# Ranges and one-hot rows of a sparse attention layer: from VectorE's comparisons to ScalarE's absolute values and positive parts

## What is computed

```python
mask = adj.astype(jnp.float32) + jnp.eye(n, dtype=jnp.float32)
q, k, v = [(h @ W.T + b).reshape(n, 8, 32) for W, b in ((Wq, bq), (Wk, bk), (Wv, bv))]
scores = jnp.einsum('nhd,mhd->hnm', q, k) / jnp.sqrt(32)
scores = jnp.where(mask[None, :, :] == 0, -1e9, scores)
attn = jax.nn.softmax(scores, axis=-1)
ctx = jnp.einsum('hnm,mhd->nhd', attn, v).reshape(n, 256)
h1 = _layer_norm(h + ctx @ Wo.T + bo, ln1_g, ln1_b)
ff = jax.nn.relu(h1 @ W1.T + b1) @ W2.T + b2
h2 = _layer_norm(h1 + ff, ln2_g, ln2_b)
```

## Time and profile before

| | us |
|---|---|
| median of 3 runs | 682.92 |
| lowest and highest of them | 676.41, 685.6 |
| the profiled execution, its own time | 665.67 |
| its span in the trace | 663.7 |
| PE busy in it | 530.3 |
| DVE busy | 478.3 |
| POOL busy | 238.9 |
| ACT busy | 170.1 |
| mean granted clock of TensorE, as a share of full speed | 0.903 |

### The profile page before, as it was taken

One profiled execution on the slowest core, in us unless ns is written; L12 is line 12 of the kernel. 1 busy time (PEld: TensorE's weight loads), 2 busy tenths in 40 slices (PEclk: granted clock), 3 DMA queues, 4 the chain that ended last, 5 costly groups with the idle time before them and its releaser, 6 DMA issues.

```text
span 663.7 us, 7651 instructions
## 1 busy us (share of the span) xinstructions
PE 530.3 (80%) x2434; PEld 420.0 (63%) x2434; DVE 478.3 (72%) x1210; ACT 170.1 (26%) x357; POOL 238.9 (36%) x368
## 2 busy tenths in 40 slices
PE   6979679886797988789889785587858598989791
PEld 5868567775466748646775672366745368577680
DVE  1659687898885997999789798989985996412000
ACT  1111122212321341242224133111213213521610
POOL 5100033634331465446452434324351524122222
PEclk9989769989698999899789998678978889999896
DMA  9974689999886689686645527066672753020100
GB/s 332 409 302 161 230 309 327 406 347 339 325 285 229 217 317 336 200 341 239 253 134 207 206 58 259 19 244 244 223 236 66 262 182 110 18 64 0 33 16 19
DMA packets 39211, 141.08 MB, mean 213 GB/s; under 512 B 4856, under 2 KB 15352, under 8 KB 35072
## 3 DMA queue, kind: packets, MB, share of 16 engines
q1 hardware_dynamic: 24176, 94.90, 38.7%
q0 software_dynamic: 13328, 43.55, 19.2%
q10 hardware_dynamic: 1664, 2.11, 1.0%
HBM read 123.74 MB, written 16.80 MB: 212 GB/s over the span
## 4 chain that ended last, share of the span: by engine, by line
PE 43%; DVE 33%; issue 8%; DMA 7%; ACT 5%; POOL 3%; DVEq 0%; POOLq 0%; ACTq 0%
PE ps L1009 12%; PE ps L1021 10%; DVE found L485 8%; PE ps L990 4%; PE ps L980 3%; DMA adj_buf<-in_adj 3%; DVE stats L1075 2%; PE ps L1555 2%; PE ps L814 2%; PE ps L1573 2%; DMA work<-q_table,row_of 2%; PE ps L777 2%; DVE slots L674 2%; PE ps L815 1%; ACT early L1065 1%
## 5 line engine op out<-in xcount | busy, mean ns | idle before, releaser
L485 DVE FIND_INDEX8 found<-ones,adj_buf 128x8 uint32<-128x4105 int32 (+19 forms) x54 | 145.2, 2689 | 0.0
L1009 PE MATMUL ps<-xT_all,w 128*128 128x512 f32 (+1 forms) x288 | 129.5, 597 | 11.1 <-ACT xT_all L1055 10.0
L1021 PE MATMUL ps<-w,xT_all 128*128 128x256 f32 x512 | 121.9, 393 | 3.6 <-ACT xT_all L1055 2.7
L1021 PEld LDWEIGHTS ps<-w,xT_all 128*128 128x128 f32 x512 | 98.8, 198 | 17.7 <-ACT xT_all L1055 3.6
L1009 PEld LDWEIGHTS ps<-xT_all,w 128*128 128x128 f32 x288 | 57.2, 208 | 60.4 <-issue 45.4
L940 POOL DMA_INDIRECT slots<-kv_table,col_of x54 | 54.2, 1004 | 63.8 <-DVE col_of L558 52.2
L1075 DVE BATCH_NORM_STATS2 stats<-ps 128x6 f32<-128x256 f32 x64 | 22.9, 419 | 64.0 <-PE ps L980 64.0
L1555 PE MATMUL ps<-early,xT_all 128*128 128x256 f32 x256 | 63.6, 413 | 6.1 <-DMA early<-in_wqkvT 6.0
L1055 ACT ACTIVATE xT_all<-ps,col_table 128x512 f32<-128x512 f32 (+1 forms) x72 | 45.4, 642 | 71.5 <-PE ps L1009 65.7
L1555 PEld LDWEIGHTS ps<-early,xT_all 128*128 128x128 f32 x256 | 53.3, 210 | 14.8 <-DMA early<-in_wqkvT 6.0
L814 PE MATMUL ps<-work,slots 128*128 128x128 f32 x160 | 34.8, 327 | 28.8 <-DVE slots L683 28.8
(11 more groups left out here) (160 smaller groups left out, 885.1 us busy)
## 6 DMA issues: line engine op xcount, KB each, us to landing
adj_buf<-in_adj SPq DMA_DIRECT2D x32, 2048.0 KB
xT_all<-in_xT SPq DMA_DIRECT2D x15, 512.0 KB, 22.0
kv_table<-slots POOLq DMA_DIRECT2D x7, 1024.0 KB, 5.0
slots<-kv_table SPq DMA_DIRECT2D x12, 512.0 KB
q_table<-slots POOLq DMA_DIRECT2D x16, 256.0 KB
out_dram<-early SPq DMA_DIRECT2D x7, 512.0 KB
q_own<-q_table SPq DMA_DIRECT2D x12, 256.0 KB
slots<-kv_table SPq DMA_DIRECT2D x8, 256.0 KB
```

The costliest lines, as they stand in the source:

```text
L485: last = nc.vector.max_index(dst, ones8[:], part)
L1009: last = nc.tensor.matmul(ps[:, q["bank"] + f % 2, 0:q["g"] * P], w1[:, k, f * P:(f + 1) * P], q["h1T"][:, k, :], start=(k == 0), stop=(k ...
L1021: nc.tensor.matmul(to, q["ffT"][:, f, j * P:(j + 1) * P], w2[:, f, :], start=(f == 0), stop=False)
```

## The change

For all batches but tile 0, ACT makes both matrices alone. Ranges: the distance as before, then max(0, distance + b) with b = 0.5 - spill/2 (so the constants of `half` at L521 change), then max(0, 1 - that), in place, each pass waiting for the one before. With half-integer distances this gives exactly 1 inside the range and 0 outside. One-hot rows: |column + 0.5 + (128 t - node number)|, the bracket being made by one new subtraction of 128xU on DVE in `cols_dve`, then max(0, 1 - that), in place. Tile 0 keeps its comparisons on DVE under new names. `rt_act` stands where `distance_act` stood; `onehot_act` stands behind the exponential of the step (in the head, behind evacuation 11). The waits of the readers follow: `lists_pe` and `ell_pe` wait for ACT's semaphores. POOL makes the constant `tile_mid` with two more instructions.

```diff
@@ spill_dve
-            nc.vector.tensor_scalar(units(half, q), units(spill, q), 0.5, -0.25, ALU.mult, ALU.add)
+            reach = (0.5, -0.25) if q.first else (-0.5, 0.5)
+            nc.vector.tensor_scalar(units(half, q), units(spill, q), reach[0], reach[1], ALU.mult, ALU.add)
@@ rt_dve, now for tile 0 alone
-        def rt_dve(dve, q):
-            dve.wait_ge(distance, q.p + 1)
+        def rt0_dve(dve):
+            q = TILE0
+            dve.wait_ge(distance, total_prepared(two_signals, q.p + 1))
...
@@ cols_dve
+            done = total_prepared(two_signals, q.p)
+            if not q.first:
+                mids = tile_mid[:, q.tiles[0]:q.tiles[0] + q.T]
+                nc.vector.tensor_tensor(row_off[q.par][:, 0:q.U], mids if q.nu == 1 else mids.to_broadcast([P, q.U]), got[:, :, q.k + 1],
+                                        ALU.subtract).then_inc(slots_ready, 1)
@@ onehot_dve, now for tile 0 alone, without its wait for acc_ps
-        def onehot_dve(dve, q):
...
+        def onehot0_dve(dve):
@@ lists_pe
-            pe.wait_ge(rt_ready, q.p + 1)
+            if q.first:
+                pe.wait_ge(scoring0, 1)
+            else:
+                pe.wait_ge(rt_ready, q.b + 1)
             pe.wait_ge(starts_ready, q.p + 1)
-            wait(pe, onehot_ready, q.p)
+            wait(pe, cols_ready, q.p)
+            if q.p == TILE0.p + 1:
+                pe.wait_ge(scoring0, 2)
@@ ell_pe
-            pe.wait_ge(onehot_ready, q.p + 1)
+            pe.wait_ge(onehot_ready, 2 * (q.b + 1))
@@ new on ACT
+        def rt_act(act, q):
+            distance_act(act, q)
+            done = total_prepared(two_signals, q.p)
+            act.wait_ge(distance, done + 1)
+            for u in range(q.U):
+                row = rt[q.par][:, u, :]
+                last = nc.scalar.activation(row, row, ACT.Relu, bias=half[:, q.u0 + u:q.u0 + u + 1])
+            last.then_inc(distance, 1)
+            act.wait_ge(distance, done + 2)
+            for u in range(q.U):
+                row = rt[q.par][:, u, :]
+                last = nc.scalar.activation(row, row, ACT.Relu, bias=ones_col[:, 0:1], scale=-1.0)
+            last.then_inc(rt_ready, 1)
+
+        def onehot_act(act, q):
+            act.wait_ge(slots_ready, total_prepared(two_signals, q.p + 1))
+            wait(act, acc_ps, q.before)
+            for u in range(q.U):
+                last = nc.scalar.activation(onehot[q.par][:, u, :], edge_mid[:], ACT.Abs, bias=row_off[q.par][:, u:u + 1])
+            last.then_inc(onehot_ready, 1)
+            act.wait_ge(onehot_ready, 2 * q.b + 1)
+            for u in range(q.U):
+                row = onehot[q.par][:, u, :]
+                last = nc.scalar.activation(row, row, ACT.Relu, bias=ones_col[:, 0:1], scale=-1.0)
+            last.then_inc(onehot_ready, 1)
@@ ACT's loop over the steps
                 if i + 1 < NB:
-                    distance_act(act, STEPS[i + 1])
+                    rt_act(act, STEPS[i + 1])
                 dense(1)
                 probs_act(act, q)
+                if i + 1 < NB:
+                    onehot_act(act, STEPS[i + 1])
@@ DVE's loop over the steps
-                if soon:
-                    rt_dve(dve, soon)
...
                 if soon:
                     cols_dve(dve, soon)
-                    onehot_dve(dve, soon)
```

More of the change, by code:

```diff
@@ L122, in total_prepared, with two_signals @@
     return sum(value(q) for q in PREPARED[:upto])
+def two_signals(p):
+    return 1 if p.first else 2
 def total_par(value, q):
@@ L170, in build @@
         row_ids = sb("row_ids", [P, TILES])
+        tile_mid = sb("tile_mid", [P, TILES])
+        row_off = [sb(f"row_off{i}", [P, 3]) for i in range(2)]
         ones8 = sb("ones8", [P, FOUND], I32)
@@ L539, in rt_dve @@
                 last = nc.vector.tensor_scalar(row, row, half[:, q.u0 + u:q.u0 + u + 1], None, ALU.is_le)
-            last.then_inc(rt_ready, 1)
+            last.then_inc(scoring0, 1)
         def cols_dve(dve, q):
@@ L547, in cols_dve @@
             nc.vector.tensor_scalar(slot, got[:, :, q.k], slot_col[:, 0:1], None, ALU.add).then_inc(slots_ready, 1)
+            done = total_prepared(two_signals, q.p)
[3 more added lines that the diff above has]
+                                        ALU.subtract).then_inc(slots_ready, 1)
             nc.vector.tensor_scalar(row_of[q.par][:, 0:q.U], got[:, :, q.k + 1], -1.0 - (q.tiles[0] // 2) * 2 * P, 0.0, ALU.add, ALU.max)
-            dve.wait_ge(slots_ready, q.p + 1)
+            dve.wait_ge(slots_ready, done + 1)
             nc.vector.tensor_tensor(hot(q), slot_no[:, 0:q.k].unsqueeze(1).to_broadcast([P, q.U, q.k]),
@@ L558, in cols_dve @@
                 nc.vector.tensor_reduce(col_of[q.par][:, 0:q.U], pick, AX_X, ALU.add).then_inc(cols_ready, 1)
-        def onehot_dve(dve, q):
+        def onehot0_dve(dve):
+            q = TILE0
             got = lists_out(q)
-            wait(dve, acc_ps, q.before)
             for u in range(q.U):
[L564 to L567, removed]
+                last = nc.vector.tensor_scalar(onehot[q.par][:, u, :], edge_mid[:], 0.5, got[:, u, q.k + 1:q.k + 2], ALU.add, ALU.is_equal)
+            last.then_inc(scoring0, 1)
         def edge_scores_dve(dve, q):
@@ L725, in below0_dve @@
             dve.wait_ge(softmax0, 2)
[L726 removed]
+            dve.wait_ge(scoring0, 4 * PIECES0 + 2)
             s = slots0()
@@ L823, in queries0_pe @@
             pe.wait_ge(own_loaded[q.par], 2 * 16)
-            pe.wait_ge(rt_ready, q.p + 1)
-            wait(pe, scoring0, 4 * i)
+            pe.wait_ge(scoring0, 4 * i + 2)
             for j in range(2):
@@ L1370, in _ @@
             nc.gpsimd.iota(row_ids[:], [[P, TILES]], base=1, channel_multiplier=1, **exact).then_inc(s_const, 1)
+            nc.gpsimd.iota(tile_mid[:], [[P, TILES]], base=0, channel_multiplier=0, **exact).then_inc(s_const, 1)
             for q in BATCHES:
@@ L1382, in _ @@
             last.then_inc(s_const, 1)
+            pool.wait_ge(s_const, CONSTS - 1)
+            nc.gpsimd.tensor_scalar(tile_mid[:], tile_mid[:], 1.0, 0.5, ALU.mult, ALU.add).then_inc(s_const, 1)
             pool.dma_start(kv_dram[0:1, :], zero_rows[0:1]).then_inc(s_pad, 16)
@@ L1476, in _ @@
                     act.wait_ge(s_const, CONSTS)
-                    distance_act(act, b0)
+                    rt_act(act, b0)
+                if i == 11:
+                    onehot_act(act, b0)
                 if i == 13:
@@ L1695, in _ @@
             find_dve(dve, b1_, 0)
-            rt_dve(dve, TILE0)
+            rt0_dve(dve)
             find_dve(dve, b1_, 1)
             cols_dve(dve, TILE0)
-            onehot_dve(dve, TILE0)
+            onehot0_dve(dve)
             listed_dve(dve, b1_)
```

14 lines of the change are left out of this document (5 added, 9 removed).

## The result

The changed kernel takes 678.2 us (median of 20 runs, 673.95 to 686.28), the kernel before 674.14 us in its 20 runs beside them; the ratio is 1.0096, with a 95% interval of 1.0062 to 1.013. (Every ratio here leaves out runs over 1.5% above the fastest of their kernel, so it differs a little from the quotient of the medians.) So the time is no more than 2% away, as forecast, but it is slower, by some 6.5 us by the ratio and 4.1 by the medians, where the sum said +0.1.

What follows compares the result with a forecast made beforehand. DVE was taken to carry the path in a group's first steps, PE in second steps and alone from 549 us. Gains and losses summed to +0.1 us on the shown median 682.92, giving 683.0 us, range 668 to 691.

Steps and rivals of the forecast that it cites:

- First steps: Steps 2, 4, 6, 8, 10: DVE carries the path, loses 0.67 us of work, sum starts earlier; 3.3 us gained.
- Second steps 3, 5, 7, 9: ACT starts ranges late, so PE's lists matmuls come later: +0.85, +0.78, +0.31, +0.84 us.
- Second steps 11 and 15, and steps 12, 13 and 16: DVE carries the path after the lists, +0.33, +0.1 us; the other three at PE's pace, -0.1, +0.1, +0.2.
- Rival B: Longer PE waits in steps 4 and 6 start two to three groups at lower clock: 691 us; chance 0.15.
- Step 17: One-hot passes delay the norm on ACT, so PE's transposes come later with nothing to hide it: +1.0 us.
- Rival A: DVE's relief is nearly all on the path: 14 us go, 669 us; chance 0.27 in whole or part.
- Rival C: ACT's waits between its own passes cost 0.40 us, not 0.04; seven steps later, +5, 688 us; chance 0.11.
- D: The change doesn't do what it says: other ACT functions could force table loads; chance 0.01.
- Head, step 0, step 1: Less DVE work in the head, -0.7 us; late ranges delay queries and gather, +0.9; ACT free in time, -0.7.

Runs made afterwards that it cites:

- E5: The changed kernel run again with nothing altered: 676.7 us, ratio 1.0055 to the kernel before.
- E4: The changed kernel, but ACT makes ranges only in first steps and for batch 0, DVE the others: 672.82 us, 0.9945 of the kernel before.
- E9: The changed kernel with ACT's range passes ahead of the second norm and feed-forward relus in steps 11, 12, 13, 15, 16: 666.02 us, 0.9919 of the kernel before.
- E1: Half of the change on the kernel before: ACT makes the one-hot rows, DVE still compares for the ranges: 673.66 us, ratio 0.9942.
- E12: E9 plus useless identity matmuls on PE ahead of the lists in steps 9, 11, 12, 13, 15: 661.47 us, 0.985 of the kernel before.
- E3: The changed kernel with one-hot passes behind norm, edge exponentials and h1 pass on ACT in seven first steps: 676.97 us, 1.0012 of the kernel before.
- E8: The changed kernel with ranges ahead of second norm and relus in every step from 3 on not first of its group: 671.85 us, 0.9958 of the kernel before.

## Why the prediction was right in its class, and where its sum failed

- **The time, 683.0 us.** It lies 4.8 us from the 678.2 measured, and that is partly luck: it stood on 682.92 us, the median of three runs, which 20 runs put 8.8 us lower, and the change was put too low by 4 to 6.5 us. The range of 668 to 691 us holds either way.
- **First steps, 0.67 us each.** Right in the mechanism. In step 4 DVE needs 13.16 us from the queries' product to the last edge weights and needed 13.89: -0.73; in steps 6, 8 and 10 it is -0.72, -0.79 and -0.79. PE no longer waits before the lists, and waits 1.24 us before L854 (L836 before), as forecast. The sum starts 0.72 us after PE is ready, where it was 0.42.
- **Second steps 3, 5, 7, 9.** Right where it can be told. In step 5 the lists follow the key product after 7.76 us and did after 6.97: +0.79 for +0.78; L797 starts 2.22 us after L884. In steps 7 and 9 it is +0.33 and +0.83 for +0.31 and +0.84; in step 3 the lists came 0.55 us sooner, behind a first step that waits for gathered rows. The steps are cut at DVE's key product, so part of PE's lateness falls into the next one: step 5 is 0.29 us longer, and in step 6 the queries come 0.61 us later. In pairs, steps 5 and 6 took +0.17 us for the sum's +0.11 (+0.95 in E5's trace), 7 and 8 -0.46 for -0.36.
- **Second steps 11 and 15, and steps 12, 13 and 16: the step that failed.** It put them at +0.33, +0.1 and -0.1, +0.1, +0.2, 0.6 us in sum, as steps in which DVE carries the path or PE its own pace. They cost 5.5 us in the traces, and 10, 14 and 17 another 6.8, where the sum had -0.67, -0.5 and +1.0. In these five steps PE's queue is empty between edge scores and lists. The lists came 0.94, 0.54, 1.27 and 2.21 us later in 11, 13, 15 and 16, and 0.12 sooner in 12, which lost 1.34 at a clock of 0.77 for 0.84. E4 and E9 take the lateness away in two ways and the stretch falls from 208 to 197.6 and 197.8 us. How the 12.3 us divide between lateness and clock, and which wait brings the clock down, is not shown: in E1, and in step 12 of E4, it was low without late ranges.
- **Rival B, the granted clock (0.15).** The 691 us at the upper end of the range, 8 over the sum, is B's, an estimate of mine from rows 10 and 11: PE's waits in steps 4 and 6 grow, and two to three groups begin at the lower clock, at the 1.6 us by which the two sums of the earlier trace rows differ for the sum and as much behind it. No run shows that term there; what the runs show is a loss with the clock, of like size, in another place. The sum of step 4 stayed high (0.49 us for its first pair, 0.39 for the others, clock 1.00), and that of step 6 fell in the first trace, after a wait of 2.00 us where it was 1.67. Its stretch, its first two pairs of L834, and the first pair of step 8:

```profile
282.70:286.00 3.30, 3.22 (x17) 3.23 (x18) 3.30 (x3) 0.00 (x0) 0.00 (x0) 0.58 1.00 421
282.78 0.49 PE L834 MATMUL ps<-work,slots 128*128 128x128 f32 x2 [2.00 <-DVE slots L697]
283.38 0.64 PE L834 MATMUL ps<-work,slots 128*128 128x128 f32 x2
340.89 0.49 PE L834 MATMUL ps<-work,slots 128*128 128x128 f32 x2 [2.33 <-DVE slots L697]
```

That put the edge scores of step 7 (L809) 1.64 us further behind the sum, as the rival said, and it cost nothing: the lists of that step start when ACT's third pass is done, 15.34 us after the sum, as in E5's trace (15.33), where the clock stayed at 1.00 after a wait of 1.78 us; before it was 15.02. Nor does the length of the wait alone decide: the last row, of step 8, has its first pair in 0.49 us after 2.33 us, where before it took 0.80 after 2.09. The clock cost time in steps 10 to 17 (0.89 before, 0.79 with the change). By E12 some 8 us of the stretch can hang on it (7.9 us; 0.7% in the ratio, at the edge of the noise). The sum carried no clock at all; here, where it lengthened waits of PE of 2 to 3 us (2.52 to 5.10 in step 11, at 0.77 and 0.65), it should have.
- **Step 17, +1.0 us.** The norm's part was right: E3 gives 0.86 us for it. The step lost 3.58 us; 1.67 more are its attention matmuls (6.99 us for 5.32; clock of the step 0.93 for 1.00), and the last 1.05 are PE's lateness from step 16.
- **Rival A (669 us)** is out by the time. DVE's relief, 14.3 us of busy time, was mostly lost in waits (L557 waits 17.3 us for the lists, L547 waited 2.1). **Rival C** is out: ACT's passes follow each other with 0.03 us between (405.98 to 406.01). **D** is out: one table load (L1505), 1.3 us, as before.
- **ACT** is busy 221.6 us and not 232: a pair takes 0.69 us, and the 232 counted single durations. **DVE** is at 464 and not 455, by the same slip: 14.3 us is the stream's 16 less 2 that the sum itself used.
- **Head, step 0, step 1**: -1.6, +6.9 and -1.1 us in the first trace, -0.4, +1.9 and -1.6 in E5's, for -0.7, +0.9, -0.7. Step 0 ends with DVE's wait for gathered rows, which varied by 5 us between two executions of one kernel; nothing can be read from it.

## What to carry to other kernels

Work moved to an idle engine starts when that engine's queue lets it; ask of each consumer what it does in the meantime, and look for steps in which it has nothing. Here the same three passes made a stretch of eight steps 207.98 us long behind a norm and evacuations and 197.82 ahead of them in five steps, for 195.65 before; ahead of them in all steps, where the norm and evacuations were needed first, part of the gain was lost (E8). And where PE's waits are already a few microseconds long, as in step 11 here (2.52 us, then 5.10, and the step's clock 0.77, then 0.65), price what a longer one may do to the granted clock of the work behind it, not only the wait.

## What the runs showed of the hardware that was not expected

Useless matmuls paid. Filling waits of 1.2 to 2.3 us with 1.3 to 3.5 us of multiplications by the identity made the 28 small matmuls behind one of them 3.28 us long and not 6.13, and the eight steps 189.96 us and not 197.82 at the same order of work; the kernel's 0.7% over E9 is at the edge of the noise. The clock of the eight steps went from 0.84 to 0.90. Step 10, which follows a filled wait and took 27.34 us as without it, shows that one filled wait doesn't always decide.

The falls of the clock repeat: steps 10 to 17 took 207.98 and 208.34 us in two profiles of the same kernel, no step more than 0.3 us apart, while step 0, which ends with a wait for gathered rows, differed by 5 us.
